# Head scores over three PSUM banks, weighed sums and their turned form in one bank

## The reference

```python
qk = einsum('bhqd,bhkd->bhqk', Q, K)              # 512 x 77 per head
p = softmax(scale * qk (+ mask))                  # layer 1: scale = 1 / (2 t), t from a small network
out = einsum('bhqk,bhkd->bhqd', p, V)             # weighed sum per head
x = x + tanh(g) * (out.reshape(...) @ Wo + bo)
```

## Time and profile before

| what | us |
|---|---|
| median of 3 runs | 1029.87 (1025.64 to 1031.05) |
| the profiled execution's own time | 1030.26 |
| its span from first to last instruction | 1028.4 |
| PE busy | 887.1 |
| DVE busy | 684.8 |
| ACT busy | 473.2 |
| mean granted TensorE clock | 0.967 of full speed |

### The profile page before, as it was taken

The page is one execution under the profiler, slowest core; times in us unless marked ns, Lnnn a source line. Parts: engine busy times, 40 slices in busy tenths (PEclk is TensorE's granted clock), DMA queues, the critical chain, the costliest instruction groups (busy, mean ns, idle before and its releaser), DMA issues.

```text
span 1028.4 us, 14302 instructions
## 1 busy us (share of the span) xinstructions
PE 887.1 (86%) x4731; PEld 597.1 (58%) x4731; DVE 684.8 (67%) x2069; ACT 473.2 (46%) x1134; POOL 119.3 (12%) x206
## 2 busy tenths in 40 slices
PE   2688999978778779779999999999999988989965
PEld 1345445433334556656677676767667666777744
DVE  3835626292765977976768678668756677777744
ACT  0375564677676565565263442443243233322312
POOL 3000100040220310310001001001000111110102
PEclk9999999988979999999999999999999999999988
DMA  6700000000000000000000000000000000000000
GB/s 177 242 1 0 2 0 2 1 0 1 0 1 1 1 1 1 1 2 1 1 1 2 1 1 1 1 1 2 1 1 1 1 1 11 1 11 1 2 10 11
DMA packets 12063, 12.70 MB, mean 12 GB/s; under 512 B 3758, under 2 KB 7896, under 8 KB 11992
## 3 DMA queue, kind: packets, MB, share of 16 engines
q1 hardware_dynamic: 9272, 9.98, 3.2%
q10 hardware_dynamic: 2336, 1.29, 0.5%
q0 software_dynamic: 384, 0.53, 0.2%
HBM read 10.75 MB, written 1.05 MB: 11 GB/s over the span
## 4 chain that ended last, share of the span: by engine, by line
PE 60%; DVE 23%; ACT 7%; issue 5%; POOL 2%; ACTq 0%; POOLq 0%; DVEq 0%
PE bank L1679 10%; PE bank L1667 6%; PE bank L1669 5%; PE bank L1668 5%; PE bank L1587 5%; PE bank L1600 4%; DVE nm L1187 3%; PE bank L1472 3%; DVE hb L1331 3%; DVE hb L1322 2%; ACT PTs L962 2%; PE bank L1644 2%; PE bank L1425 2%; PE bank L1650 2%; PE bank L1725 2%
## 5 line engine op out<-in xcount | busy, mean ns | idle before, releaser
L999 ACT ACTIVATE hb<-bank 96x512 f32<-96x512 f32 (+1 forms) x160 | 95.1, 594 | 208.5 <-PE bank L1669 208.0
L1679 PEld LDWEIGHTS bank<-m_w,hb 128*128 128x128 f32 (+1 forms) x1280 | 166.6, 195 | 23.2 <-issue 5.5
L1667 PE MATMUL bank<-parts,m_w_lo 128*96 128x512 f32 (+1 forms) x320 | 152.5, 477 | 31.1 <-DVE hb L1322 22.6
L1679 PE MATMUL bank<-m_w,hb 128*128 128x128 f32 (+1 forms) x1280 | 176.3, 282 | 2.3 <-DVE hb L1322 2.1
L1331 DVE SCALAR_TENSOR_TENSOR hb<-hb,bank 96x512 f32<-96x512 f32 (+1 forms) x160 | 109.0, 681 | 93.4 <-ACT hb L999 92.5
L1669 PE MATMUL bank<-parts,m_w_hi 128*96 128x512 f32 (+1 forms) x320 | 127.8, 399 | 0.0
L1668 PE MATMUL bank<-parts,m_w_hi 128*96 128x512 f32 (+1 forms) x320 | 127.4, 398 | 0.0
L1322 DVE TENSOR_TENSOR hb<-hb,bank 96x512 f32<-96x512 f32 (+1 forms) x160 | 109.8, 686 | 10.4 <-PE bank L1669 4.9
L1667 PEld LDWEIGHTS bank<-parts,m_w_lo 128*96 128x96 f32 (+1 forms) x320 | 59.4, 186 | 78.0 <-DVE hb L1322 34.1
L1600 PE MATMUL bank<-Qs,KT 112*77 112x512 f32 x192 | 93.7, 515 | 11.1 <-ACT PTs L962 8.9
L1484 PE MATMUL bank<-KT,Qs 96*128 96x308 f32 x192 | 77.5, 428 | 13.4 <-ACT PTs L908 8.0
(11 more groups left out here) (271 smaller groups left out, 1502.3 us busy)
## 6 DMA issues: line engine op xcount, KB each, us to landing
m_w_raw<-in_L_ffn_w_dram SPq DMA_DIRECT2D x2, 1024.0 KB, 6.6
m_w<-in_L_ffn_W_dram SPq DMA_DIRECT2D x1, 1408.0 KB, 9.5
x<-in_x_dram ACTq DMA_DIRECT2D x4, 256.0 KB, 6.4
out_dram<-x SPq DMA_DIRECT2D x4, 256.0 KB, 2.0
f_out<-in_L_ffn_Wout_dram POOLq DMA_DIRECT2D x8, 64.0 KB, 3.5
m_w_raw<-in_L_ffn_W_experts_dram SPq DMA_DIRECT2D x1, 512.0 KB, 11.0
ctxn<-in_ctx_dram ACTq DMA_DIRECT2D x4, 38.5 KB
Wq<-in_L_xattn_Wq_dram SPq DMA_DIRECT2D x2, 64.0 KB
```

Of the source, the lines that this page charges most:

```text
L999: act.activation(hb[n % 3][0:m, :], bank[UP[u, n]][0:m, :], ACT.Tanh, scale=0.5).then_inc(*chunk_act.up(u, n))
L1667: pe.matmul(dst, w_lo, x_hi, start=True, stop=False)
L1679: op = pe.matmul(bank[7][:, t * P:(t + 1) * P], hb[n % 3][0:m, t * P:(t + 1) * P], wd, start=i == 0 and t == 0, stop=ends_expert(k, n) and ...
```

## The change

The scores of head h go to bank h % 3 in place of h % 2. `weigh`, `copy_out`, `turn` and `divide` all use bank 3 (`HEADS`) for every group, in place of banks 2 and 3 in turn. The number, order and size of the instructions stay; only banks and the waits that follow from them differ.

```diff
--- before.py
+++ after.py
@@ -625,6 +625,7 @@
     S1 = S0 + NS
     RING = (1, 0, 2, 3)
     TURN = (4, 5)
+    HEADS = 3
     EARLY = 6
     XA = {"A3": 2, "F3": 2}
     LATE = 1
@@ -859,7 +860,7 @@
                     act.wait_ge(*out_turned.at(u, g - 2))
                 elif g == 0 and u[1]:
                     act.wait_ge(*result_psum.at(("A", u[1] - 1)))
-                act.activation(Os[:, g % 2, :], bank[2 + g % 2][:], ACT.Copy).then_inc(*out_kept.up(u, g))
+                act.activation(Os[:, g % 2, :], bank[HEADS][:], ACT.Copy).then_inc(*out_kept.up(u, g))
 
             def pre(u):
                 half, s, k, b = u[0], side(u), kind(u), stream(u)
@@ -959,7 +960,7 @@
                             act.wait_ge(*out_psum.at(u, (h - NPT) // J))
                         if l == 1:
                             act.wait_ge(*temp_vector.at(u, "invt"))
-                        act.activation(PT[h % NPT][0:S2, :], bank[h % 2][0:S2, :], ACT.Exp,
+                        act.activation(PT[h % NPT][0:S2, :], bank[h % 3][0:S2, :], ACT.Exp,
                                        scale=invt[:, 2, h:h + 1] if l == 1 else ROOT,
                                        bias=mk[b][:, 2:3] if l == 2 else 0.0).then_inc(*probs_ready.up(u, h))
                         if h % J == 0 and h:
@@ -1059,7 +1060,7 @@
                 dve.wait_ge(*out_turned.at(u, g))
                 if g == 0 and u[1]:
                     dve.wait_ge(*att_turned.at(("A", u[1] - 1)))
-                turned = bank[2 + g % 2][:].rearrange("p (t j c) -> p t j c", t=T, j=J)
+                turned = bank[HEADS][:].rearrange("p (t j c) -> p t j c", t=T, j=J)
                 dve.reciprocal(rden[:, g], turned[:, :, :, HD]).then_inc(*out_divided.up(u, g, "inv"))
                 dve.wait_ge(*out_divided.at(u, g, "inv"))
                 dve.tensor_tensor(att[:, :, 32 * g:32 * g + 32].rearrange("p t (j d) -> p t j d", d=HD),
@@ -1419,12 +1420,12 @@
 
             def turn(u, g):
 
-                free(2 + g % 2)
+                free(HEADS)
                 pe.wait_ge(*out_kept.at(u, g))
                 for t in range(T):
-                    op = pe.transpose(bank[2 + g % 2][:, t * P:(t + 1) * P], Os[:, g % 2, t * P:(t + 1) * P], ident[:])
+                    op = pe.transpose(bank[HEADS][:, t * P:(t + 1) * P], Os[:, g % 2, t * P:(t + 1) * P], ident[:])
                 op.then_inc(*out_turned.up(u, g))
-                reader[2 + g % 2] = (out_divided, u, g)
+                reader[HEADS] = (out_divided, u, g)
 
             def pre(u):
                 half, s, k, y = u[0], side(u), kind(u), stream(u)
@@ -1580,18 +1581,18 @@
 
                     def weigh(g):
 
-                        free(2 + g % 2)
+                        free(HEADS)
                         for j in range(J):
                             h = g * J + j
                             pe.wait_ge(*probs_ready.at(u, h))
-                            op = pe.matmul(bank[2 + g % 2][32 * j:32 * j + 32, :], VP[:, h, :], PT[h % NPT][0:S2, :],
+                            op = pe.matmul(bank[HEADS][32 * j:32 * j + 32, :], VP[:, h, :], PT[h % NPT][0:S2, :],
                                            start=True, stop=True, tile_position=(0, 32 * j))
                         op.then_inc(*out_psum.up(u, g))
-                        reader[2 + g % 2] = (out_kept, u, g)
+                        reader[HEADS] = (out_kept, u, g)
 
                     def scores(h):
 
-                        b = h % 2
+                        b = h % 3
                         free(b)
                         dst = bank[b][0:S2, :]
                         if l == 0:
```

## The result

The kernel after takes 1021.72 us (median of 15 runs, 1017.34 to 1026.43) against 1029.64 of the kernel before in 15 runs beside it. The ratio is 0.9937, 95% interval 0.9922 to 0.9953: 4.8 to 8.0 us faster, 6.5 in the middle. The forecast was 1026.2, that is 3.8 us faster, with 0.58 on "within 0.5%". The time lies in the range, 0.2 us inside its fast end of 1021.5, and outside the 1023 to 1028.5 that the forecast gave itself; the win is 0.63%, just past the 0.5%.

A forecast was written before the change was run, and what follows sets the result against it. PE was taken as the bound, with 16.2 us of waits before scores as the prize. Three score banks win 12.8 us, the shared bank loses 9.0: 3.8 us won, 1026.2 us forecast, range 1021.5 to 1033.0.

The forecast's parts named there:

- What bounds the kernel: PE is the bound; its 16.2 us in 28 waits for exponentials before scores are the whole prize.
- Part 2: One bank for sums and turned form: weigh waits for the previous divide in ten of 36 pairs; 9.0 us lost.
- that chain hangs on ACT and PE, so it slips with PE and both prices stay: Units 6 and 7: DVE's work before divide slips with PE, so 1.34 and 0.93 us stay lost, 2.27 a unit.
- Units 0 to 5: Bodies of units 0 to 5, both parts of the change together: 7.5 us won.
- ACT itself is the slow one: Start of units 0 and 1: ACT's exponentials limit the scores, so about 4.0 of 5.2 us are won.
- the new wait of the turn for copy_out: Units 4 and 5: turn(1) finds copy_out still running, so 0.77 of a 0.90 us wait is won.
- Units 6 and 7: Second wait, 0.76 us, worth nothing because a down product waits for DVE's L1322; 1.0 a unit won from the scores.
- The third wait of these units: Units 6 and 7: the third wait before scores, 0.2 us, goes.
- part 1: Scores over three banks in units 0 to 9: 12.8 us won of 16.2 us of waits for exponentials.
- (a): Rival, units 6 to 9: DVE catches up, half of part 2's loss gone; 8.3 us won, 1021.6; chance 0.20.
- (b): Rival, units 0 to 5: ACT or copy_out takes over freed waits; 1.1 to 3.1 us slower, 1031 to 1033; chance 0.16.
- (c): Rival, weigh(1) to weigh(3) beside experts: divide's end stays, wins become longer waits; 5.9 us slower, 1036; chance 0.14.

The follow-up runs named there:

- the shared bank alone: Kernel before with every group's sums and turned form in bank 3, scores still over two banks: 1043.35 us, ratio 1.0147; repeated: 1042.98 us, ratio 1.0135.
- the second profile: The kernel after run again unchanged, beside the kernel before: 1022.07 us, ratio 0.9944.
- two sum banks: Against the kernel before: scores over three banks, using whichever sum bank is free, group sums in banks 3,2,3,2: 1016.44 us, ratio 0.9884; repeated: 1014.64 us, ratio 0.9867.

## Why the prediction was right, and where it was off

**What bounds the kernel:** right. PE's waits before the scores were the prize, and all but 2.4 of 16.2 us went.

**Part 2**, with its ten shortfalls: right in place and size. The loss was forecast at 9.0 us and is 8.8 in the bodies with the shared bank alone; the waits are 9.4 in the kernel after. The claim "that chain hangs on ACT and PE, so it slips with PE and both prices stay" held: in unit 6 the waits are 1.25 and 0.82 us, forecast 1.34 and 0.93 with the hand-over. The hand-over itself is 0.05 us in all ten places (377.73 to 377.78 in the rows below), not 0.09.

**Units 0 to 5:** forecast 7.5 won net; from the table, with unit 5 from the second profile, 2.0 + 1.9 + 1.0 + 1.0 + 1.3 + 1.4 = 8.6. "ACT itself is the slow one" in units 0 and 1 and the new wait of the turn for copy_out in unit 4 (0.18 us in the kernel after) both hold.

**Units 6 and 7: the step that failed.** "The second, 0.76 at 385.15, doesn't pay: behind it on PE stands a down product at 385.88, and DVE's L1322, which feeds it, ends at [...] 385.88." Forecast for the two units together 2.5 us lost; measured 0.1 won. The kernel after shows it; PE's rows of unit 6, then DVE's gate product (L1323 here) and divide:

```profile
374.12 0.62 PE L1601 MATMUL bank<-Qs,KT 112*77 112x512 f32 x2
...
374.58 0.60 PE L1426 MATMUL bank<-ident,Os 128*128 128x128 f32 x4
...
375.02 1.06 PE L1680 MATMUL bank<-m_w,hb 128*128 128x128 f32 x8
...
377.78 1.07 PE L1588 MATMUL bank<-PTs,VP 77*32 77x512 f32 x8 [1.25 <-DVE att L1066]
...
375.30 0.69 DVE L1323 TENSOR_TENSOR hb<-hb,bank 128x512 f32<-128x512 f32 x1
...
377.44 0.29 DVE L1066 TENSOR_TENSOR att<-bank,rden 128x128 f32<-128x128 f32 x1
```

The down product starts at 375.02, before the gate product that was said to feed it has even started, at 375.30. The code says why: `down(n - LATE)` with `LATE = 1` multiplies the chunk before, whose gate product was done a chunk ago. Two ends at 385.88 were a coincidence, and I read a dependency from it that the profile had not named: no releaser stands on the row of L1679 in the earlier trace rows. The wait of this down product for L1322, one of the forecast's own signs of being right, never came.

**At its place a wait is worth more than its idle gap.** The same place sizes it. PE's rows before and behind the wait in the kernel before, around the row of 385.15 in the earlier trace rows:

```profile
384.00 0.39 PE L1600 MATMUL bank<-Qs,KT 112*77 112x512 f32 x1
...
385.45 0.60 PE L1425 MATMUL bank<-ident,Os 128*128 128x128 f32 x4
```

From the start of scores(6) to the turn it is 1.45 us; in the kernel after, 374.12 to 374.58, 0.46. So 0.99 was won by a gap of 0.76. The gap is counted from the modelled end of scores(6), 384.39, where without a wait the next matmul would have started 0.23 after its start, at 384.23; and the matmul behind the wait took 0.30 to the next start, not 0.23. That is 0.16 + 0.07. The third wait of these units, 0.2, was likewise worth 0.43 (4.77 to 4.34 us between weigh(2) and weigh(3)). The forecast counted the gaps alone. It counted part 2 rightly, by start times. So per unit 0.99 for a wait taken as nothing and 0.23 more for the third make up 2.4 of the 2.6 us by which units 6 and 7 were off. With the 2.6 the forecast's 3.8 would have been 6.4. Units 0 to 5 won 1.1 more than said and 8 and 9 lost 0.2 more (1.4, forecast 1.2), which makes the bodies' 7.3.

That does not make a body shorter by more than its gaps everywhere, for another wait can take part of it back. Unit 8's first scores in the kernel before, around the row of 513.16 in the earlier trace rows, then with two sum banks (L1602 scores, L1669 up product, PEld its weight load):

```profile
511.49 0.70 PE L1600 MATMUL bank<-Qs,KT 112*77 112x512 f32 x2
...
513.46 0.40 PE L1667 MATMUL bank<-parts,m_w_lo 128*128 128x512 f32 x1
```

```profile
504.47 0.94 PE L1602 MATMUL bank<-Qs,KT 112*77 112x512 f32 x3
...
505.25 0.39 PE L1669 MATMUL bank<-parts,m_w_lo 128*128 128x512 f32 x1
...
508.27 0.19 PEld L1669 LDWEIGHTS bank<-parts,m_w_lo 128*128 128x128 f32 x1 [0.46 <-ACT xff L872]
```

From the first scores to the product behind them it is 0.78 us in place of 1.97: 1.19 won by the gap of 0.97. But 3 us later PE waits for ACT's copy L872, and the body is only 0.86 shorter. Over all units the two things nearly cancel. The bodies won 7.3 us with both parts and lost 8.8 with part 2 alone, so part 1 was worth about 16.1, if the parts add up as they do in units 6 and 7. That is the whole 16.2 us of gaps in the earlier trace rows, where the forecast, by what it took off in units 0 to 7, came to 12.8.

**Rivals.** (a), that DVE catches up, is out: the waits for the divide are 9.4, not below 5. Its time, 1021.6, is the measured one for another reason: part 1 was worth 3.3 us more, not part 2 less. The range reached down to that time to hold (a), so that it held the measured one is luck. (b) is out: the bodies of units 0 to 5 are 8.6 us shorter. (c), the weigh as meeting point of PE and DVE: that they meet there in units 6 to 9 is so, and the forecast had it too. What (c) added, that the divide stays where it is when PE comes earlier, is out: PE reaches weigh(1) of unit 6 1.8 us earlier in the body in the kernel after than with the shared bank alone, and waits 1.25 us there against 1.23. The Trainium skill's rule (Perfetto Trace Analysis, Matmuls) that groups should rotate through banks holds for both halves here: rotating the scores over three won, rotating the sums over two in addition won some 5.5 us more (two sum banks), and taking the sums' rotation away by itself cost 8.8 us in the bodies; its extreme, every weigh exposed, did not come, ten of 36 did.

**The clock** was given 2.6 us either way. In the bodies of the profiled pair it gave 2.6 us of 9.9; in the shared bank alone it took some 3 us of the profile's 13.0, and at most 6.8 on the average of the runs.

## What to carry to other kernels

Size a wait of PE by start-to-start times around it, not by the idle gap of the row, and then look for the next wait behind it, which may take a part back. Before a freed wait is written off because another operand ends at the same moment, find in the code which iteration's operand it is. Where two buffers alternate with gaps in their use, lend the one that is free at the moment to the hungrier ring, rather than giving one away for good: 12 us in place of 6.5 here, at no cost in memory.

## What was not expected of the hardware

The granted clock differed by kernel, and did so again in a second set of runs. With the shared bank alone twelve executions had 0.956 to 0.967, the kernel before 0.962 to 0.972 in the 32 beside them, and about 6 us beyond the bodies' 8.8 came along with it, of which the clock can be shown to hold some 3. A fall of 3.4 us cost 1.6 us where PE had no gap. The stretch from 213 to 310 us, layer 1's statistics with F0 beside them, is a tenth of the span and holds a third to a half of the time at the lower level in the profiles (27 to 40 us of 63 to 87 in those of the kernel before, the kernel after and the shared bank alone). Whether PE's added waits cause the further falls was not settled.
